# Cross-attention and a quantised FFN on one core: maxima transposed earlier, norms behind the residual, one maximum of g a slot

## The reference

```python
def attention(h, kv_c):                         # h = layernorm(x), 64 sequences
    q_big  = einsum('bshk,hkq->bshq', (h @ Wq.T).reshape(b, s, 16, 128), w_kc_q)
    kv     = kv_c * cos + rotate_half(kv_c) * sin
    scores = einsum('bhsr,bhlr->bhsl', q_big @ W_qr, kv @ W_kr)
    ctx_c  = einsum('bhsl,bld->bhsd', softmax(scores), kv)
    return einsum('bhsd,hkd->bshk', ctx_c, w_kc_kv).reshape(b, s, -1) @ Wo.T

def bitlinear(x, w):                            # weights to -1, 0, 1; rows to 8 bits
    xn    = x / max(norm(x), 1e-12) * sqrt(d)
    scale = 127 / clip(max(abs(xn)), 1e-5)
    return (clip(round(xn * scale)) / scale) @ ternary(w).T

x = x + attention(layernorm(x), ctx)
x = x + bitlinear(gelu(bitlinear(layernorm(x), w1)), w2)
```

## Time and profile before

| | |
|---|---|
| median of 3 runs | 459.38 us (455.22, 459.38, 459.72) |
| the profiled execution | 457.08 us |
| its span, first to last instruction | 454.9 us |
| mean granted clock of TensorE | 0.957 |
| TensorE matmuls | 393.1 us busy (86%) |
| VectorE | 330.5 us (73%) |
| ScalarE | 257.8 us (57%) |
| GpSimd | 255.2 us (56%) |

### The profile page before, as it was taken

One profiled execution on the slowest core, in us unless ns is written; L12 is line 12 of the kernel. 1 busy time (PEld: TensorE's weight loads), 2 busy tenths in 40 slices (PEclk: granted clock), 3 DMA queues, 4 the chain that ended last, 5 costly groups with the idle time before them and its releaser, 6 DMA issues.

```text
span 454.9 us, 8971 instructions
## 1 busy us (share of the span) xinstructions
PE 393.1 (86%) x2855; PEld 282.0 (62%) x2870; DVE 330.5 (73%) x873; ACT 257.8 (57%) x477; POOL 255.2 (56%) x321
## 2 busy tenths in 40 slices
PE   9799889794988999989999999999999997876554
PEld 7587557572665776767676767676767674464222
DVE  0364867584798789887878787878787888877564
ACT  1155543332667676675758585858585857556340
POOL 1209447994365656667373738373837373767543
PEclk9899999996999999999999999999999999999665
DMA  8993254443213232424262434252424253443333
GB/s 216 404 333 128 56 142 117 119 117 92 64 52 78 62 79 71 102 48 106 73 107 71 108 73 105 72 107 71 108 72 107 72 107 77 102 127 81 78 97 92
DMA packets 65533, 48.81 MB, mean 107 GB/s; under 512 B 50384, under 2 KB 55888, under 8 KB 65104
## 3 DMA queue, kind: packets, MB, share of 16 engines
q1 hardware_dynamic: 64880, 44.72, 37.8%
q10 hardware_dynamic: 608, 3.54, 2.3%
HBM read 31.98 MB, written 4.46 MB: 80 GB/s over the span
## 4 chain that ended last, share of the span: by engine, by line
POOL 34%; issue 31%; PE 15%; DMA 7%; DVE 6%; SPq 4%; ACT 1%; POOLq 1%; ACTq 0%; DVEq 0%
POOL cl L440 7%; POOL tq L463 6%; POOL qb L466 6%; POOL xa L455 3%; DMA wq_s<-wq 3%; POOL xq L458 3%; POOL yc L450 2%; POOL xn L315 2%; PE hps L786 2%; POOL w_s L478 2%; SPq L365 2%; DMA shift<-nmax 2%; PE ps L744 2%; PE ps L690 2%; DVE cr L953 1%
## 5 line engine op out<-in xcount | busy, mean ns | idle before, releaser
L440 POOL TENSOR_TENSOR cl<-cr,ch 128x512 fp32r<-128x512 f32 x64 | 80.3, 1277 | 131.0 <-ACT ch L550 131.0
L690 PE MATMUL ps<-xh,ah 128*128 128x256 f32 x256 | 75.6, 295 | 4.9 <-ACT g L565 4.5
L754 PE MATMUL hps<-bh,ch 128*128 128x256 f32 x256 | 76.7, 300 | 1.4 <-POOL cl L440 1.4
L534 ACT ACTIVATE qf<-ps 128x512 f32<-128x512 f32 x64 | 37.5, 586 | 65.4 <-PE ps L692 65.4
L755 PE MATMUL hps<-bl,ch 128*128 128x256 f32 x256 | 72.2, 282 | 0.0
L756 PE MATMUL hps<-bh,cl 128*128 128x256 f32 x256 | 72.2, 282 | 0.0
L691 PE MATMUL ps<-xl,ah 128*128 128x256 f32 x256 | 71.9, 281 | 0.0
L692 PE MATMUL ps<-xh,al 128*128 128x256 f32 x256 | 71.8, 280 | 0.0
L550 ACT ACTIVATE ch<-cr 128x512 fp32r<-128x512 f32 x64 | 39.3, 631 | 55.0 <-DVE cr L953 55.0
L690 PEld LDWEIGHTS ps<-xh,ah 128*128 128x128 f32 x256 | 48.2, 188 | 26.7 <-issue 25.8
L786 PE MATMUL hps<-w2q,qt 128*128 128x256 bf16 x256 | 39.1, 303 | 17.3 <-DMA qt<-qb 12.8
(11 more groups left out here) (136 smaller groups left out, 830.2 us busy)
## 6 DMA issues: line engine op xcount, KB each, us to landing
rb<-rinv_d SPq DMA_DIRECT2D x64, 256.0 KB, 3.9
xs<-x SPq DMA_DIRECT2D x8, 512.0 KB, 4.3
out<-yo SPq DMA_DIRECT2D x32, 128.0 KB, 3.5
wq_s<-wq SPq DMA_DIRECT2D x2, 1024.0 KB, 14.4
w_s<-w_t SPq DMA_DIRECT2D x2, 1024.0 KB, 7.2
wo_s<-wo_t ACTq DMA_DIRECT2D x1, 2048.0 KB, 11.1
wk_a<-wk_t SPq DMA_DIRECT2D x2, 512.0 KB, 7.3
kvs<-kvn SPq DMA_DIRECT2D x8, 128.0 KB, 4.1
```

Of the source, the lines that this page charges most:

```text
L440: pool.tensor_tensor(cl[:, u % 2, :, b * S:(b + 1) * S], cr[:, :, b * S:(b + 1) * S], ch[:, u % 2, :, b * S:(b + 1) * S].bitcast(F32), ALU ...
L690: pe.matmul(o, ah[:, c, cols], xh[:, k % 2, c, :], start=(c == 0), stop=False)
L754: pe.matmul(O[:, 0:D], c_h, bh[:, hp, :], start=(hp == 0), stop=False)
```

## The change

On TensorE `turned(n)` (and with it, where an even slot has an `up`, the first half of `project`) moves ahead of queries or projection. On SP `shift_rows(n)` moves ahead of `turn_g(n-10)` in odd slots. On GpSimd the reciprocal deviations move from the front of even slots to the back of odd slots (of slot 4 in one case), and `g_round` waits for a scale of its own tile. On VectorE `x_max` moves behind `row_max` and `row_sum`, `norms` behind `residual`; `g_max` and `g_scale` are made for one tile in each slot instead of two in each even slot; and the statistics are spread by a table over slots 2 to 11, ahead of the quadrant sums.

```diff
--- before.py
+++ after.py
@@ -215,6 +215,8 @@
                     dve.wait_ge(sem["bn_stats"], t)
                     dve.bn_aggr(mv[:, t - 1, :], st6[:, (t - 1) % 4, :]).then_inc(sem["bn_means"], 1)
 
+        STATS = (8, 10, 12, 15, 18, 21, 24, 26, 28, 30, 32)
+
         def reciprocal_deviations(pool, part):
 
             c = slice(4 * part, 4 * part + 4)
@@ -411,10 +413,10 @@
                     if n % 2 == 0 and tile(n - 6):
                         turn_x(n - 6)
                         turn_x(n - 5)
+                    if tile(n):
+                        shift_rows(n)
                     if n % 2 and tile(n - 10):
                         turn_g(n - 10)
-                    if tile(n):
-                        shift_rows(n)
                     if n == 0:
                         sp.dma_start(w2_s[:, :, :], w2_t.rearrange("(a p) n -> p a n", p=P)).then_inc(sem["w2_loaded"], 16)
                     if 1 <= n < 7:
@@ -458,7 +460,7 @@
                     pool.tensor_scalar(xq[:, t % 2, :], xa[:, :], 1.0, -MAGIC, ALU.mult, ALU.add).then_inc(sem["x_rounded"], 1)
 
                 def g_round(t):
-                    pool.wait_ge(sem["g_scale_steps"], 2 * (t // 2 + 1))
+                    pool.wait_ge(sem["g_scale_steps"], 2 * (t + 1))
                     at_least(pool, sem["g_rounded"], t)
                     pool.tensor_scalar(tq[:, :], g[:, t % GB, :], c2[:, t:t + 1], MAGIC, ALU.mult, ALU.add).then_inc(sem["g_scaled"], 1)
                     pool.wait_ge(sem["g_scaled"], t + 1)
@@ -504,8 +506,6 @@
                     if n in (0, 1):
                         pool.wait_ge(sem["end_made"], 1)
                         rope(pool, n + 2, sem["rope_steps"]).then_inc(sem["rope_done"], 1)
-                    if n % 2 == 0 and 4 <= n < 16:
-                        reciprocal_deviations(pool, n // 2)
                     if n % 2 == 0 and tile(n - 6):
                         x_round(n - 6)
                         x_round(n - 5)
@@ -516,6 +516,8 @@
                         ctx_lo(n - 2, 1)
                     if tile(n - 3):
                         centre(n - 3)
+                    if n == 4 or n % 2 and 7 <= n < 16:
+                        reciprocal_deviations(pool, n // 2)
                     if n % 2 == 0 and tile(n + 4):
                         norm_x(pool, n + 4)
                         norm_x(pool, n + 5)
@@ -873,17 +875,21 @@
                     if n % 2 == 0 and tile(n - 7):
                         up(n - 7, 0)
                         up(n - 7, 1)
+                        if tile(n - 3):
+                            project(n - 3, 0)
+                        if n <= NT:
+                            turned(n)
                     if k < NB:
                         queries(k, b)
                     if n % 2 and k + 1 < NB:
                         x_t(pe, k + 1)
+                    if (n % 2 or not tile(n - 7)) and n <= NT:
+                        turned(n)
                     if n == 3:
                         pe.wait_ge(sem["b_lo_done"], HP // 2)
                     if tile(n - 3):
-                        project(n - 3, 0)
-                    if n <= NT:
-                        turned(n)
-                    if tile(n - 3):
+                        if n % 2 or not tile(n - 7):
+                            project(n - 3, 0)
                         project(n - 3, 1)
                     if 0 < n < 3:
                         fold_out(n + 1)
@@ -974,11 +980,11 @@
                     dve.wait_ge(sem["gelu_done"], 2 * t + 2)
                     dve.tensor_reduce(gscale(amax, t), g[:, t % GB, :], AX.X, ALU.max, apply_absolute_value=True).then_inc(sem["g_maxima"], 1)
 
-                def g_scale(p):
-                    c = slice(2 * p, 2 * p + 2)
-                    dve.wait_ge(sem["g_maxima"], 2 * p + 2)
-                    dve.scalar_tensor_tensor(out=gm[:, c], in0=amax[:, p + 2, 2:4], scalar=FLOOR2, in1=level[:, 2:4], op0=ALU.max, op1=ALU.mult).then_inc(sem["g_scale_steps"], 1)
-                    dve.wait_ge(sem["g_scale_steps"], 2 * p + 1)
+                def g_scale(t):
+                    c = slice(t, t + 1)
+                    dve.wait_ge(sem["g_maxima"], t + 1)
+                    dve.scalar_tensor_tensor(out=gm[:, c], in0=gscale(amax, t), scalar=FLOOR2, in1=level[:, 2:3], op0=ALU.max, op1=ALU.mult).then_inc(sem["g_scale_steps"], 1)
+                    dve.wait_ge(sem["g_scale_steps"], 2 * t + 1)
                     dve.reciprocal(c2[:, c], gm[:, c]).then_inc(sem["g_scale_steps"], 1)
 
                 def norms(j):
@@ -1073,14 +1079,12 @@
                     if tile(n):
                         quadrant_max(n, 0)
                         quadrant_max(n, 1)
-                    if tile(n - 4):
-                        x_max(n - 4)
-                    if n % 2 == 0 and 0 <= (n - 6) // 2 < NB + 2:
-                        norms((n - 6) // 2)
                     if tile(n):
                         row_max(n)
                     if tile(n - 1):
                         row_sum(n - 1)
+                    if tile(n - 4):
+                        x_max(n - 4)
                     if tile(n - 2):
                         divide(n - 2, 0)
                         divide(n - 2, 1)
@@ -1088,18 +1092,21 @@
                         x_lo(dve, k + 1)
                     if tile(n - 3):
                         residual(n - 3)
+                    if n % 2 == 0 and 0 <= (n - 6) // 2 < NB + 2:
+                        norms((n - 6) // 2)
                     if n % 2 and tile(n - 5):
                         x_scale((n - 5) // 2)
-                    if n % 2 == 0 and tile(n - 8):
+                    if tile(n - 8):
                         g_max(n - 8)
-                        g_max(n - 7)
-                        g_scale((n - 8) // 2)
-                        if tile(n - 10):
+                        g_scale(n - 8)
+                        if n % 2 == 0 and tile(n - 10):
                             finish(n - 10)
                     if n in (0, 2):
                         w_means(n // 2)
                     if n < 2:
                         ternary(n)
+                    if 2 <= n < 12:
+                        statistics(dve, STATS[n - 2], STATS[n - 1])
                     if tile(n):
                         quadrant_sum(n, 0)
                         quadrant_sum(n, 1)
@@ -1109,8 +1116,6 @@
                         b_lo(0)
                     if n < 3:
                         b_lo(n + 1)
-                    if 2 <= n < 14:
-                        statistics(dve, 4 + 2 * n, 6 + 2 * n)
 
 
 # ---- launch: one core ----
```

## The result

| | before | after |
|---|---|---|
| median | 458.54 us (455.22 to 459.72, 4 runs) | 504.31 us (500.17 to 511.04, 4 runs) |
| the profiled execution | 457.08 us | 503.3 us |
| its span | 454.9 us | 501.2 us |
| mean granted clock of TensorE | 0.957 | 0.925 |

The ratio is 1.098, 95% interval 1.088 to 1.108; the run of 511.04 us, a disturbed one, is left out of it. The change makes the kernel slower by about 46 us, 11 less than the 57 of the prediction.

A forecast was written before the change was run, and what follows sets the result against it. TensorE bounded it before; after, VectorE, its norms held by GpSimd. 38.7 + 0.9 + 4.5 + 5.6 + 4 + 4 - 1.8 + 0.8 = 56.7 us more: 514 or 516, said 515; range 468 to 540.

The forecast's parts named there:

- TensorE's part: Main loop: TensorE alone reaches the odd `turned` at S + 13.9, the next S 8.0 later, 21.9 us a pair.
- S: Start of an even slot's scores on TensorE, from which times within a pair of slots are counted in us.
- When the norms start and when GpSimd starts: Even slots: norms begin at S + 6.8, `ctx_lo` at S + 8.0, with seven norm instructions through by then.
- The collision: Even slots: norm instructions pass only between GpSimd's, mostly one a joint; norms end at S + 13.4 instead of 9.5.
- rival A: Even slots, milder: two norm instructions pass at each joint, pair 24.2 us, total 472; chance 0.15 with what lies between.
- The odd `turned`: Odd slots: `turned` comes at S + 18.0, TensorE stands 4.1 us ahead of it, and the pair is 26.0 us.
- The clock: Behind TensorE's stand in each pair: a lower granted clock adds 1.5 us, so a pair takes 27.5.
- Slots 8 and 9, 28 and 29: The pairs just outside slots 10 to 27: +4.5 us for 8 and 9, +5.6 us for 28 and 29.
- Slot 30 and the tail: Slot 30, norms meeting GpSimd almost from the first: +4 us; tail, finish behind the norms of slot 32: +4 us.
- Early slots: Slot 6 shorter by 1.8 us, slot 3 longer by 0.8 as `turned` meets unfinished quadrant maxima; early -1.0.
- The small edits: Reciprocal deviations: -1.8 us in slot 6; slot 3 +0.8; shift rows cost nothing themselves; statistics within VectorE's spare time.
- rival B: Even slots, faster: GpSimd doesn't hold the norms, a pair is 22.1 us, total 446; chance 0.14.

The follow-up runs named there:

- Version 1: The changed kernel with the norms alone put back ahead of the row maximum: 443.0 us, ratio to before 0.972.
- experiment 2: The changed kernel with two of the norms' small arrays in PSUM and three copies a call added: 457.05 us, ratio to before 1.0015.
- experiment 5: The changed kernel with twelve unneeded matmuls ahead of the transposition of each odd slot from 9 on: 491.89 us, ratio to before 1.077.
- Experiment 7: Version 1 with TensorE's order of before, `turned` late again: 458.01 us, ratio to before 1.004.
- experiment 6: Version 1 with the maxima of g and their scale again two at a time in even slots: 444.48 us, ratio to before 0.973.

## Why the prediction was right, and where its terms were off

The direction, the cause and the chain of steps held; the time was 515 against 504.3, within the range.

- **TensorE's part, 21.9 us a pair alone:** right. Version 1 runs at 21.6 to 21.9. The even `turned` is at S + 3.3 and the way from the odd one to the next scores 7.89 us for my 8.0.
- **When the norms start and when GpSimd starts:** S + 6.86 for my 6.8, `ctx_lo` S + 7.94 for my 8.0 (slot 18). Through before it: six for my seven.
- **The collision:** right, and shown by experiment 2 to hang on the SBUF inputs. The norms ended at S + 13.1 to 13.5 in six of the nine even slots 12 to 28, for my 13.4. In slots 12, 16 and 22 they ended at S + 12.0. There the last ones pass: between the short tensor_scalars two get through at a joint, as rival A had it, between the two `cl` one, as I had it. What decides is close: in slot 18 L201 began 0.06 us behind `yc` and was held, in slot 22 it began 0.05 us behind and passed. I can't settle what tells these apart.
- **The odd `turned`:** on the mean of slots 10 to 26 at S + 17.26 for my 18.0, so I had 0.7 us too much a pair.
- **The clock:** 1.5 us behind a stand is right where the clock falls (9.41 - 7.89). In seven pairs experiment 5 filled most of the stand, and the loss was gone. But it is not paid in every pair (not in those of slots 10 and 22), and the length of the stand doesn't tell in which (3.44 us without it in slot 11, 1.9 us with it in experiment 5), so I had the price right, and when it is due I can't say: on the mean the way is 9.03, not 9.5, another 0.5 a pair. The two together are the mis-sized term: 26.3 for 27.5 us a pair, 9 x 1.2 = 11 of the 12 us by which the 39.6 that I summed for slots 10 to 27 exceed the 27.7 measured.
- **Slots 8 and 9, 28 and 29:** +4.0 and +5.7 for +4.5 and +5.6.
- **Slot 30 and the tail:** +11.3 (90.4 us from the start of slot 30 to the end, for 454.9 - 375.8 = 79.1) for my +8. Up to the transposition of slot 32 it is +4.5 for my +4, with TensorE standing 7.7 us in slot 31. Behind it it is +6.8 for my +4: I had counted one projection behind the finish, but the whole chain of norms, 6.7 us in slot 32, is on the path there.
- **Early slots:** -2.4 up to slot 7 for my -1.0. Slot 6 is 1.7 us shorter for my 1.8; slots 2 to 5 gained 1.1 together, which I hadn't counted. In that, slot 3 lost 0.2, not 0.8.
- **The small edits:** costs of about nothing, as said; but so were the gains. Experiment 7 measures them all, with the norms in front and the transposition late, at 1.004 of before.

The terms on hand sum to 35.0 at the start of slot 30 and 11.3 behind it, 46.3 us, which is the difference of the spans.

The sentence of the Trainium skill that VectorE instructions with two SBUF inputs contend with GpSimd ones that read SBUF ("SBUF — State Buffer", "Who interferes with whom") agrees with the trace: those of 0.16 us were held up to 1.2. By issue order the norms, which begin first, could have kept the pair of ports; the trace speaks against that for a chain of short instructions: `cl` starts at 258.91 while L201 still runs, and all 64 of them keep a median of 1.28 us. So rival B had no ground. Its 446 is close to the 443.0 of version 1 by chance, since that is another kernel. With the norms unheld in their new place experiment 2 took 457: a pair was 22.5 to 22.6 us in slots 12 to 27, slots 8 and 9 took 24.3 where rival B had 21.9, and from slot 30 to the end it was 83.2 us where B had 77.9.

## What to carry to other kernels

- A chain of tiny VectorE instructions with two SBUF inputs was cheap here only where GpSimd was quiet. Before moving it, lay it on GpSimd's timeline: each 1.28 us instruction of GpSimd that it met held one of its 0.16 us until it ended, and at the joints of the short ones, of 0.5 us, up to two got through. If the chain must stand there, try one operand of each in PSUM; here that took 47 us off.
- An edit that helps can be hidden under one that hurts. Undo the parts one at a time, in pairs where they could act on each other; here that turned a kernel 10% slower into one 3% faster.
- Where TensorE stands for another engine, count the slower matmuls behind the stand too. Matmuls that nobody needs, put into the stand, took some 10 us off.

## What the hardware showed that I hadn't expected

- A tensor_scalar from SBUF to SBUF, with one tensor input, is held like those with two (L196: 0.17 us median, 1.20 longest), while a reciprocal and a reduction from SBUF to SBUF never are (L988: 163 to 165 ns in 32 occurrences). A tensor_scalar that writes PSUM isn't held either (163 to 167 ns).
- The collision costs GpSimd next to nothing: `cl` has a median of 1276 ns before and 1278 after. The short instruction pays nearly all of it.
- The scale of g, an instruction of 0.16 us with two SBUF inputs, is held too when it is made for each tile: in version 1, slots 10 to 27, it takes 0.76 us on the mean (L986, 18 instructions). VectorE is busy 10.4 us more there than before (179.30 for 168.88), and it costs no time that shows: with pairs again (experiment 6) it is busy 166.69 us and the kernel as fast.
